# Two maxima on rows 0 and 32, each into its half of a zeroed buffer, in place of a maximum and a product with the head mask

## The reference, cut to what matters

```python
# x: (16, 1024, 256); 16 heads of 16; layer norm, attention with relative positions, then a routed FFN
x = x + layernorm(attn(layernorm(x)))
x = x + layernorm(ffn(layernorm(x)))
# attn
qk  = einsum('bhld,bhrd->bhlr', q, k) / sqrt(16)
qk += einsum('bhld,lrd->bhlr', q, rel_emb[r - l + 511])
att = softmax(qk, axis=-1)
out = lin(einsum('bhlr,bhrd->bhld', att, v))
```

## Time and profile before

| | |
|---|---|
| median of three runs | 6341.79 us (6341.11 to 6344.4) |
| the profiled execution: its time, its span | 6342.86 us, 6341.1 us |
| mean granted TensorE clock | 0.985 of 2.4 GHz |
| TensorE matmul busy, weight load busy | 5961.8 us (94%), 5617.6 us (89%) |
| VectorE busy | 4987.0 us (79%) |
| ScalarE, GpSimd busy | 3127.8 us (49%), 3652.9 us (58%) |

### The profile page before, as it was taken

One profiled execution on the slowest core, in us unless ns is written; L12 is line 12 of the kernel. 1 busy time (PEld: TensorE's weight loads), 2 busy tenths in 40 slices (PEclk: granted clock), 3 DMA queues, 4 the chain that ended last, 5 costly groups with the idle time before them and its releaser, 6 DMA issues.

```text
span 6341.1 us, 408511 instructions
## 1 busy us (share of the span) xinstructions
PE 5961.8 (94%) x178176; PEld 5617.6 (89%) x178176; DVE 4987.0 (79%) x10289; ACT 3127.8 (49%) x5145; POOL 3652.9 (58%) x4709
## 2 busy tenths in 40 slices
PE   5999999999999999999999999999999999999997
PEld 4989899899998998898999899899999999998987
DVE  3787788878788887878887888888788788887786
ACT  1555455455555554555555555455555555554554
POOL 5555655565565555555655655555565556556555
PEclk7999999999999999999999999999999999999998
DMA  3111121111212112121121211112111121211211
GB/s 87 39 44 52 36 61 36 54 44 38 60 36 62 36 36 62 36 61 34 42 58 36 60 37 49 47 40 60 36 53 45 36 60 40 59 37 36 62 36 27
DMA packets 570090, 296.74 MB, mean 47 GB/s; under 512 B 384177, under 2 KB 534689, under 8 KB 568625
## 3 DMA queue, kind: packets, MB, share of 16 engines
q1 hardware_dynamic: 568624, 272.86, 16.0%
HBM read 184.46 MB, written 88.60 MB: 43 GB/s over the span
## 4 chain that ended last, share of the span: by engine, by line
PE 83%; DVE 8%; issue 4%; DVEq 3%; POOLq 1%; ACT 1%; POOL 0%; SPq 0%; DMA 0%
PE sc L667 22%; PE pw L693 15%; PE sc L683 14%; PE sc L662 13%; PE pm L714 4%; PE pw L700 4%; PE pw L714 4%; PE pm L674 4%; DVE r L962 3%; DVEq L973 2%; DVE y2n L928 2%; DVE nm L971 1%; PE pm L727 1%; PE pm L705 1%; DVE gate L1005 1%
## 5 line engine op out<-in xcount | busy, mean ns | idle before, releaser
L962 DVE TRANSPOSE_TENSOR_REDUCE r<-sc 128x32 f16<-128x1024 f32 x2048 | 2548.8, 1245 | 52.0 <-PE sc L667 51.4
L667 PE MATMUL sc<-rm,tw 96*128 96x32 f16 x65536 | 2293.4, 177 | 71.6 <-issue 70.8
L847 ACT ACTIVATE prob<-sc 128x1024 f32<-128x1024 f32 x2048 | 2097.3, 1024 | 193.7 <-PE sc L683 141.3
L667 PEld LDWEIGHTS sc<-rm,tw 96*128 96x128 f16 x65536 | 1979.9, 97 | 79.5 <-issue 79.0
L662 PE MATMUL sc<-qm,ks 96*128 96x64 f16 x32768 | 1639.8, 193 | 28.8 <-DMA ks<-qk_s 15.5
L971 DVE TENSOR_REDUCE nm<-pm 16x32 f16<-16x256 f32 x2048 | 840.8, 411 | 753.7 <-PE pm L674 750.3
L662 PEld LDWEIGHTS sc<-qm,ks 96*128 96x128 f16 x32768 | 1302.8, 98 | 34.3 <-issue 34.2
L683 PE MATMUL sc<-nmm,pick 128*128 128x64 f16 x32768 | 1302.0, 193 | 2.5 <-DVE nmm L974 1.2
L683 PEld LDWEIGHTS sc<-nmm,pick 128*128 128x128 f16 x32768 | 1151.9, 98 | 122.4 <-issue 105.5
L693 PE MATMUL pw<-prob,vs 128*32 128x128 f32 x32768 | 1115.7, 277 | 129.8 <-DVE nm L971 124.7
L693 PEld LDWEIGHTS pw<-prob,vs 128*32 128x32 f32 x32768 | 842.6, 110 | 185.8 <-DVE nm L971 137.4
(11 more groups left out here) (131 smaller groups left out, 5803.9 us busy)
## 6 DMA issues: line engine op xcount, KB each, us to landing
raw<-qk_s SPq DMA_DIRECT2D x774, 64.0 KB, 2.8
tw<-tw_s SPq DMA_DIRECT2D x512, 72.0 KB, 2.1
v_s<-vpad SPq DMA_DIRECT2D x136, 256.0 KB, 3.6
vs<-v_s SPq DMA_DIRECT2D x64, 512.0 KB, 3.7
ks<-qk_s SPq DMA_DIRECT2D x384, 64.0 KB, 2.5
xin<-x SPq DMA_DIRECT2D x138, 128.0 KB, 2.9
qk_s<-qkh SPq DMA_DIRECT2D x272, 64.0 KB, 1.7
qk_s<-qkl SPq DMA_DIRECT2D x272, 64.0 KB, 1.6
```

Of the source, the lines that this page charges most:

```text
L667: last = mm(out3[:, :, 2 * k:2 * k + 2], tw[:, jp, u:u + P], rm[:, i, k, :, :], start=False, stop=False, skip_group_check=True)
L847: A(prob[:, jp % 2, :, :, i * IW:(i + 1) * IW], sc[:, 2 * buf:2 * buf + 2, :].rearrange("p c (h i) -> p c h i", i=IW), ACT.Exp).then_inc(s ...
L962: v.tensor_reduce(r1[:, 0:2 * H], sc[:, 2 * buf:2 * buf + 2, :].rearrange("p c (h i) -> p (c h) i", i=IW), axis=AX.X, op=ALU.max, apply_tr ...
```

## The change

`maxima` writes the two chunks' maxima into separate 128-column halves of r1, heads 0 to 7 at columns 0 to 7 and heads 8 to 15 at columns 32 to 39, so that the transpose puts them on rows 0 to 7 and rows 32 to 39 of p_max. `spread` has no drain and no product: two reductions, each over 32 rows, write the first half of nmm from rows 0 to 31 and the second half from rows 32 to 63. nmm is now 128 x (2, 2, 128), double-buffered over jp, and its other rows stay zero from the start. mask_h, nm and s_nmr are gone. TensorE's wait ahead of `mixed` is on s_nm, which comes with the second reduction. The transpose at k = 1 is two accumulating products with `heads`, a 128 x 16 matrix that takes rows 0 to 7 and 32 to 39 to the 16 heads. `shift` reads its 64 columns from nmm as two runs of 32.

```diff
-        r1 = sb("r1", [P, H + P], f16)
-        nm = sb("nm", [P, 2, P], f16)
-        nmm = sb("nmm", [P, 2, IW], f16)
+        r1 = sb("r1", [P, 2, P], f16)
+        nmm = sb("nmm", [P, 2, 2, P], f16)
+        heads = sb("heads", [P, H], f16)
...
-            for h0 in (0, half_h):
+            for h0 in (0, 32):
                 g.affine_select(out=pick[:, :, :], in_=pick[:, :, :], compare_op=ALU.not_equal, fill=1.0,
                                 base=-h0, pattern=[[-1, half_h], [0, P]], channel_multiplier=1)
                 pool.drain()
-            keep(mask_h[:, 0, :], ALU.is_ge, half_h - 1, [[0, IW]], -1)
-            keep(mask_h[:, 1, :], ALU.is_ge, -half_h, [[0, IW]], 1)
+            for s in range(2):
+                part = heads[:, s * half_h:(s + 1) * half_h]
+                g.affine_select(out=part, in_=part, compare_op=ALU.not_equal, fill=1.0, base=-32 * s,
+                                pattern=[[-1, half_h]], channel_multiplier=1)
...
-                    last = mm(p_max[:, c * P:(c + 1) * P], r1[:, c * H:c * H + P], ident16[:, :], start=True, stop=True)
+                    last = mm(p_max[:, c * P:(c + 1) * P], r1[:, c, :], ident16[:, :], start=True, stop=True)
...
-                        last = mm(pairs[:, :, h, :], pick[:, h, :], nmm[:, :, :],
+                        last = mm(pairs[:, :, h, :], pick[:, h, :], nmm[:, jp % 2, :, i * IW:(i + 1) * IW],
...
-                    mm(p_n[:, 0:H], nm[:, (jp - 1) % 2, :], ident16[:, 0:H], start=True, stop=True)\
-                        .then_inc(s_nmtp, 1)
+                    for s in range(2):
+                        last = mm(p_n[:, 0:H], nmm[:, (jp - 1) % 2, s, :], heads[:, :], start=(s == 0), stop=(s == 1))
+                    last.then_inc(s_nmtp, 1)
...
-                        pe.wait_ge(s_nmr, t * NG + g)
+                        pe.wait_ge(s_nm, t * NG + g)
...
-                v.tensor_reduce(r1[:, 0:2 * H], sc[:, 2 * buf:2 * buf + 2, :].rearrange("p c (h i) -> p (c h) i", i=IW),
+                v.tensor_reduce(r1[:, :, 0:64].rearrange("p c (s h) -> p c s h", s=2)[:, :, :, 0:H // 2],
+                                sc[:, 2 * buf:2 * buf + 2, :].rearrange("p c (h i) -> p (c h) i", i=IW),
                                 axis=AX.X, op=ALU.max, apply_transpose=True).then_inc(s_rmax, 1)
...
-                part = nm[0:H, jp % 2, i * IW:(i + 1) * IW]
-                v.tensor_reduce(part, p_max[0:H, :].rearrange("h (q i) -> h i q", i=IW), axis=AX.X, op=ALU.max,
-                                negate=True).then_inc(s_nmr, 1)
-                dve.drain()
-                v.tensor_tensor(nmm[0:H, :, :], part.rearrange("h (a i) -> h a i", a=1)
-                                .to_broadcast((H, 2, IW)), mask_h[:, :, :], ALU.mult).then_inc(s_nm, 1)
+                for s in range(2):
+                    rows = slice(32 * s, 32 * s + 32)
+                    last = v.tensor_reduce(nmm[rows, jp % 2, s, i * IW:(i + 1) * IW],
+                                           p_max[rows, :].rearrange("h (q i) -> h i q", i=IW), axis=AX.X, op=ALU.max,
+                                           negate=True)
+                last.then_inc(s_nm, 1)
```

More of the change, by code:

```diff
@@ L63, in sandwich_kernel @@
         pick = sb("pick", [P, H // 2, P], f16)
-        mask_h = sb("mask_h", [H, 2, IW], f16)
         mask_q = sb("mask_q", [ROWS, H, IW], f16)
@@ L258, in sandwich_kernel @@
         s_vst = sem("s_vst")
-        s_nmr = sem("s_nmr")
         s_oT2 = sem("s_oT2")
@@ L494, in _ @@
             g.memset(pick[:, :, :], 0.0)
-            g.memset(mask_h[:, :, :], 1.0)
+            g.memset(heads[:, :], 0.0)
             g.memset(mask_q[:, :, :], 1.0)
@@ L502, in _ @@
             g.memset(vpad[:, :, :], 1.0)
-            g.memset(nmm[:, :, :], 0.0)
-            g.memset(nm[:, :, :], 0.0)
-            g.memset(r1[:, :], 0.0)
+            g.memset(nmm[:, :, :, :], 0.0)
+            g.memset(r1[:, :, :], 0.0)
             pool.drain()
@@ L673, in transpose_max, with shift @@
                 for c in range(2):
-                    last = mm(p_max[:, c * P:(c + 1) * P], r1[:, c * H:c * H + P], ident16[:, :], start=True, stop=True)
+                    last = mm(p_max[:, c * P:(c + 1) * P], r1[:, c, :], ident16[:, :], start=True, stop=True)
                 last.then_inc(s_maxT, 1)
-            def shift(buf, g_count):
+            def shift(g, buf, g_count):
+                jp, i = divmod(g, NI)
                 pe.wait_ge(s_nm, g_count)
@@ L826, in tile @@
                     if old:
-                        shift(buffer(ph, g - 1), t * NG + g)
+                        shift((g - 1) % NG, buffer(ph, g - 1), t * NG + g)
             passes(pe, tile)
```

## The result

The changed kernel takes 6876.8 us in the median of four runs (6876.2 to 6882.2), against 6343.1 us (6341.1 to 6353.1) before: ratio 1.084, 95% interval 1.083 to 1.086. (The kernel before had a fourth run by then.) Forecast were 6832 us, 6700 to 6980. The profiled execution took 6876.5 us, 1.7 of it outside its span.

The account below looks back on a forecast made before the run. TensorE, busy 94%, was taken as the bound. Added waits of 470 us (127.5 x 3.69) and 20 us for the small transposes on 6342.9 gave 6833, set at 6832 us against the median; range 6700 to 6980.

Parts of the forecast that it names:

- g = 15: Last group of a tile: VectorE's lateness from the held-up product goes, so PE's wait changes by -0.10 us a tile.
- g = 0: First group of a tile: transposes of xn stand ahead, mixed starts at T + 1.00, so PE waits 0.19 us more.
- g = 6: Group where PE already waits, VectorE being late with the router's comparisons: wait grows from 0.46 to 0.88 us, 0.42 more.
- part C: Transpose of the maxima at k = 1 becomes two matmuls: 0.04 us each, 20 us in all, bounds 0 and 46.
- Where PE waits: Ahead of mixed, on s_nm from the second reduction: PE goes on at T + 1.19; 3.69 us a tile, 470 us.
- The step of 0.42: Time from first to second reduction's start on VectorE, taken as 0.42 us, the middle of 0.34 and 0.50.
- the low bound: Reductions starting 0.34 us apart, as overlapping neighbours do: eleven groups lose 0.08 us less each, 112 us less; 6710 us.
- Part B: VectorE's first reduction to next maximum grows from 0.74 to 0.83 us: 180 us more VectorE time, lying in its idle time.
- Part D: Maximum L962 writing four runs of eight and shift reading two runs of 32: no cost; shift's bounds -10 and +10 us.
- the clock: Rival, chance 0.13: longer waiting in g = 6 drops TensorE's granted clock once or more a tile, 180 us more: 7010.
- The vanished interference: Rival, chance 0.03: VectorE no longer meets GpSimd; with reductions almost together, 54 us goes at g = 15: 6309 us.
- The queue: Rival, chance 0.04: PE has work in hand beyond the wait, leaving only the small transposes' cost: 6363 us, +0.3%.

Follow-up runs that it names:

- the run on rows 0 to 31: Changed kernel with both reductions reading and writing rows 0 to 31, so the output differs: 6724.7 us, ratio 1.059.
- the run with wide first: Changed kernel without the wait ahead of mixed where mixed does nothing, and with wide ahead of wait and mixed in every group: 6615.6 us, ratio 1.044.
- the wait alone: Kernel before with only TensorE's wait ahead of mixed moved from s_nmr to s_nm, the product's signal: 6729.0 us, ratio 1.061.
- VectorE's time alone: Kernel before with one more small VectorE reduction behind the product in each group, which nobody waits for: 6574.5 us, ratio 1.035.

## Why the prediction was right

The mechanism was right: PE's wait moved to a signal that comes 0.4 us later, in the eleven groups that were listed, and the run with one reduction shows that without the second reduction nothing is lost. That the sum came within 45 us is in part luck, since terms that were too small (g = 15, g = 0) stood against terms that were too large (g = 6, g = 2). How much longer each group became, by the distance from T to the next T, in the mean over the tiles:

| groups | forecast, us | measured, us |
|---|---|---|
| g = 2, 14 | 0.36 each | 0.23, 0.38 |
| g = 3, 4, 7, 10, 11, 12 | 0.41 each | 0.41 to 0.43 each |
| g = 6 | 0.42 | 0.17 |
| g = 15 | -0.10 | 0.22 |
| g = 0 | 0.19 | 0.43 |
| g = 8 | 0 | 0.06 |
| g = 1, 5, 9, 13 (part C) | 0.04 each | 0.02 to 0.04 each |

- *Where PE waits* was right, group by group, and the ordinary stalls within 0.02 us: T + 1.21 for T + 1.19. (In g = 2 some tiles stood waiting for other things before, so that its mean gained less than its 0.38.) From the first to the last L971 of the kernel before there are 6178 us (116.1 to 6294.1), from the first to the last L974 now 6709 (115.6 to 6824.4): 4.15 us a tile more, where 3.69 and 0.16 for the small transposes make 3.85. 0.30 us in 128 tiles is 38 of the 45 us by which the forecast was low.
- *The step of 0.42* was taken as the middle of two rows; it is 0.42 to 0.43. By the rule of the Trainium skill that the prediction named it worked out at 0.41, and the run on rows 0 to 31 bears out that rule. That run also shows what the low bound would have been: 6725 us, near the 6720 that the sum gives with a step of 0.34. (The prediction's 6710 to 6950 for both ends of the step should have been 6720 to 6944 by its own sum.)
- *g = 15 and g = 0* were the mis-sized terms: -0.10 and 0.19 forecast, +0.27 and +0.52 in the tile shown (less for g = 0 in each third tile, where the loop's return delays PE first). Both had one cause that I had looked away from: I counted GpSimd's interference with the product as gone (240 us) and took the side work's durations as given. It moved. y2n went from 877 to 1166 ns and xn of x from 377 to 1144.

The trace shows GpSimd as the other party. Its two products with a mask around the same time as the two slow normalisations of the timeline above:

```profile
3098.81 1.15 POOL L534 TENSOR_TENSOR rm<-raw,mask_r 96x512 f16<-96x512 f16 x1
...
3101.93 1.15 POOL L534 TENSOR_TENSOR rm<-raw,mask_r 96x512 f16<-96x512 f16 x1
```

y2n ends at 3100.11, 0.15 us behind the end of the first, and xn at 3103.22, 0.14 behind the end of the second. It is so in nearly every tile: in 127 of 128 xn of x is slow, and in nine tenths of them it ends 0.149 to 0.152 us behind the end of that product; the xn of 2065 ns in the run with wide first ends 0.148 to 0.150 us behind another instruction of GpSimd, of 2.04 us. A duration that GpSimd did not set would not follow its ends like that. By the Trainium skill ("SBUF — State Buffer", section "Who interferes with whom") the engine that issues first keeps the shared pair of ports for its whole instruction and the other is blocked; the trace agrees for these two, which start 0.12 and 0.14 us behind GpSimd's. In the run with wide first the slow xn starts 0.01 us ahead of the instruction behind which it ends, so the order is not shown there. No run took GpSimd's work away to see it from the other side.

- *g = 6* was mis-sized the other way, 0.42 forecast and 0.10 measured, since the interference left the comparisons (1115 to 198 ns) and went to the gate (370 to 1035 ns), which comes out shorter by 0.25 us. The reduction there starts at T + 1.14 in the mean, not at T + 1.43.

```profile
L929 DVE TENSOR_SCALAR y2n<-y,mv,rs 128x256 f32<-128x256 f32 x128 | 149.3, 1166 | 1.0 <-POOL rs L542 1.0
L929 DVE TENSOR_SCALAR xn<-x,mv,rs 128x256 f32<-128x256 f32 x128 | 146.4, 1144 | 2.2 <-issue 2.2
L1007 DVE TENSOR_SCALAR gate<-eg,rg 128x6 f32<-128x6 f32 x128 | 132.5, 1035 | 9.9
...
L1013 DVE TENSOR_TENSOR cgt<-gate 128x36 f32<-128x36 f32 x128 | 25.3, 198 | 0.0
```

- *Part B*, VectorE's own time, was too small, and at no cost for the wrong reason. From the first reduction to the maximum there are 0.87 us, not 0.83, because the maximum too is held (its rows begin at 0 again); leaving out g = 0, the mean went from 0.725 to 0.873, 0.15 x 2048 = 303 us and not 180. And this time seems free only as long as PE's new waits slow the groups down and so give VectorE room: take most of the waits away and 333 us remain, 55 of them in the wait at g = 12; add the time without the waits and 223 us appear. With the wait alone at 388 us and VectorE's time alone at 223 us for a larger dose (0.21 us a group in the mean against 0.15), 534 us is less than their sum, so the two costs seem to hide each other in part. The doses are not those of the changed kernel, so by how much is not shown.
- *Part C*: L683 starts 0.06 behind the first of the two L728 (3014.20 to 3014.26), 0.04 before. Over all 512 the mean is 64 ns against 39: 0.025 us, 13 us in all instead of 20. Part D's terms are invisible, as the ordinary groups of the run with one reduction show.
- *The rivals*: the clock did not fall more often, 0.988 in the mean against 0.985. The vanished interference brought no gain, since it came back elsewhere. The queue covers nothing: PE starts 0.06 us behind the second reduction's end (3002.55 + 0.84 = 3003.39, to 3003.45).

## What to carry to other kernels

Before moving a wait from an early signal to a late one, measure how far the early one is from being late: here it was 0.06 us ahead of value products and nothing elsewhere, so that what went beyond it was paid in each of the eight ordinary groups of a tile. When work that met another engine is removed, ask which instruction will meet that engine next, and whether that one is on the path. A reduction over 16, 32 or 64 rows of 256 elements took 411, 414 or 415 ns here, so halves on separate rows are two instructions at the full price each.

## What was not expected of the hardware

Two reductions of 0.41 us whose rows begin at 0 and at 32 start 0.43 us apart, two that begin on the same rows 0.34; 152 us of 6877 hang on that, with the lateness that follows from it. And VectorE's normalisation over 128 x 256 elements went from 377 to 1144 ns in one place and from 381 to 2065 ns in another, in kernels whose difference lay elsewhere, by the moment at which it fell.
